# A two-layer vision transformer on one core: rounded values turned in another bank one tile later, and three queues reordered

## The chip, the cores and the metric

The kernel runs on one core of a Trainium2 chip. The metric is the device time of one execution in microseconds (us). A core has five engines with a queue each, which take their instructions in order: TensorE (PE: matrix products, and turns, that is transposes), VectorE (DVE), ScalarE (ACT), GpSimd (POOL), and SyncE (SP), which here only starts transfers. They wait for each other through semaphores. SBUF is the memory on the chip, PSUM the eight banks into which TensorE writes.

## What is computed

32 images are cut into 36 patches each and embedded; with two class tokens this makes 38 rows of 256 numbers per image. Two layers follow, each an attention and a network, with a layer norm before each:

```python
h = concat(cls_tok, cls_token, patches @ W.T + b) + pos_embedding
h = h + attn0(layernorm(h))   # a = 1 + s + s*s/2, causal, o = (a @ v) / (sum(a) + 1e-6), y = o @ Wo.T
h = h + ffn0(layernorm(h))    # x and weight rounded in blocks of 32 to a 4-bit grid, then x_q @ w_q.T + bias
h = h + attn1(layernorm(h))   # softmax attention with biases, causal, 16 heads of 16
h = h + ffn1(layernorm(h))    # gelu((x @ U1) @ V1 + b1) @ U2 @ V2 + b2
```

The rounding to the grid (per block of 32: the power of two below the largest value gives the scale, each value is rounded with the step of its own exponent) is what `scales`, `grid`, `round_to_grid` and `quantised` do for the first network, whose product is `product`.

## The kernel before

Three images make a tile of 114 rows, so there are NT = 11 tiles. Everything from the embedding on is worked tile by tile, and each engine has its own hand-written order of steps, in a function `layer0()` and a function `attention()` per engine. The loops run over tiles; at tile t an engine does steps of several stages for tiles around t. Nothing but these orders and the semaphores sets what runs when.

**First layer** (some 60 to 160 us). Per tile TensorE does `scores0(t+1)`, `values0(t)` (weights times values), `sums0(t)` (the sums of the weights, into z), `k_proj0`, `product(t-4)` of the first network, four tiles behind (LAG = 4), `v_proj0`, `q_proj0`, `out_proj0(t)` and `turn0` (the next normed tile). ScalarE does `square` (the weights), `take_z`, `add_one`, `ffn_norm(t-1)` (the norm that goes into the network), the copies `take_k0`, `take_v0`, `take_q0`, `take_hnT0` out of PSUM, and `norm0`. VectorE does `residual0(t-1)`, its half of `mask_weights(t+1)`, `divide(t)` and `ffn_residual(t-4)`; GpSimd the other half of `mask_weights` and the small steps to 1/sqrt of the variance (`rstd_0_step`, `rstd_f_step`).

The network's rounding goes by pairs of tiles p = (2p, 2p+1), six of them (NP = 6, the last has one tile). VectorE: `scales(p)` and `grid(p)`; GpSimd: `round_to_grid(p)`, two operations, and `add_ffn_bias(p)`; VectorE: `quantised(p)`, which writes the rounded values xq in bf16; TensorE: `turn_quantised(p)`; ScalarE: `take_xT(p)`, the copy from PSUM to xqT; TensorE: `product(2p)` and `product(2p+1)`; VectorE: `ffn_residual`, which adds them. In the first layer this is done for p = 0 to 3, in the second for p = 4 and 5.

The turned values of p = 0 to 3 share bank 4 with the products of `k_proj0` and `q_proj0`. So `k_proj0(t+2)` waits until they have been copied out (f_xT), and the turn stands at the end of the odd tile 2p+3:

```python
X16 = [bank[4].bitcast(bf16), bank[6].bitcast(bf16)]
pe.wait_ge(lay[0]["s_sb"], min(2 * p + 6, NT))    # in turn_quantised: q of the next tile copied out of bank 4
```

**Seam** (tiles 9 and 10 of the first layer). Instead of the next tile of the first layer, the engines do the first steps of the second: `m_proj`, `v_proj`, `s_proj` (keys, values, queries), `take_m`, `take_v`, `take_s`, `attn_norm`; GpSimd `expand(i)` (keys spread over the heads, mX) and `values_now(i)`; VectorE `keep(0)` (mask, maximum, difference) and `spread(0)`; ScalarE `weigh(0)` (the exponential). Tile i = 2 is turned into a bank that holds the values of tile 1, so that turn waits for `take_v(1)`, which waits for `values_now(0)`.

**Second layer** (some 165 to 275 us). At tile t TensorE does `scores(t+1)`, a `product`, `turn_p(t, 0..3)` (the weights, L1489), `m_proj(t+2)`, `s_proj(t+2)`, at t = 2 and 4 `turn_quantised(4)` and `(5)`, `values(t)`, `v_proj(t+2)`, `turn(t+3)`, `out_proj(t)`. VectorE does `keep(t+1)` (L1052, L1058, L1060), residuals, `spread(t+1)` (sum, reciprocal, three products L1073), `take_v(t+2)`, and the network's steps between them. `values(t)` waits for `residual(t-1)`.

## Time and profile before

| | |
|---|---|
| Time of the kernel before | 323.95 us, median of 3 runs (322.25 to 326.37) |
| The profiled execution | 326.31 us, of which the span from first to last instruction is 324.6 |
| Busy share of the span | TensorE 83%, VectorE 66%, GpSimd 53%, ScalarE 47% |
| Mean granted clock of TensorE | 0.95 of full |
| The chain that ended last | TensorE 43%, VectorE 28%, issue 9%, GpSimd 6%, ScalarE 6% |

Stages in the profiled execution: patches and embedding to 59 us, first layer to 165, second attention to 276, second network to the end. A busy share is an average over stages with different limits; which engine is waited for at the end of a stage is read from the timelines.

### The profile page before, as it was taken

Reading aid. Unit: us, or ns where it says so; the run is one execution under the profiler, and the core shown is the slowest. Engines: PE = TensorE matmul, PEld = TensorE weight load, DVE = VectorE, ACT = ScalarE, POOL = GpSimd, SP = SyncE. Lnnn points to the kernel's source line nnn. Section 1 sums busy time; section 2 is a strip of 40 time slices with the busy share of each in tenths; the row PEclk is TensorE's granted clock in tenths of the full one; section 3 lists DMA queues with packets and bytes.
Section 4 is the critical chain, followed back from the end, with each engine's and each line's share of the span. In section 5 each row is a group of like instructions: output and inputs, shape, how many; then the busy total and the mean of one; then the engine's idle time right before and its main releaser. Section 6 shows DMA issues by size and latency. Waiting matters only on the chain.

```text
span 324.6 us, 6978 instructions
## 1 busy us (share of the span) xinstructions
PE 270.3 (83%) x2720; PEld 209.0 (64%) x2720; DVE 215.1 (66%) x389; ACT 151.4 (47%) x313; POOL 171.7 (53%) x238
## 2 busy tenths in 40 slices
PE   1779899679997979798779749888999956799893
PEld 1668788558876858587668638777888844333331
DVE  0626375116698998999869998999999991422121
ACT  2312111469886858676236515543555442143541
POOL 7233335134677797979756566476776631601000
PEclk9999999799999999999979998999999995579998
DMA  6798500000000000000000000000000000001011
GB/s 178 185 267 253 128 1 3 0 0 5 2 0 2 2 2 2 1 5 0 2 0 2 2 1 3 3 0 2 0 2 2 3 0 0 3 0 31 27 60 38
DMA packets 9742, 9.87 MB, mean 30 GB/s; under 512 B 4037, under 2 KB 8878, under 8 KB 9710
## 3 DMA queue, kind: packets, MB, share of 16 engines
q1 hardware_dynamic: 9294, 9.42, 10.8%
q8 instruction: 22, 0.36, 0.5%
q14 instruction: 10, 0.08, 0.1%
q10 hardware_dynamic: 416, 0.01, 0.1%
HBM read 8.18 MB, written 1.25 MB: 29 GB/s over the span
## 4 chain that ended last, share of the span: by engine, by line
PE 43%; DVE 28%; issue 9%; POOL 6%; ACT 6%; SPq 4%; DMA 3%; ACTq 0%; POOLq 0%; DVEq 0%
PE psum L1236 8%; PE psum L1272 5%; DVE big L1073 5%; PE psum L1489 3%; PE psum L1603 3%; PE psum L1434 3%; DMA img<-in_x 3%; DVE img L988 3%; PE psum L1614 3%; SPq L323 2%; DVE st L942 2%; DVE xq L1029 2%; PE psum L1587 2%; DVE big L981 2%; PE psum L1504 2%
## 5 line engine op out<-in xcount | busy, mean ns | idle before, releaser
L1272 PE MATMUL psum<-hnT,a 128*128 128x114 f32 x352 | 50.7, 289 | 3.3 <-ACT mT L679 1.8
L1272 PEld LDWEIGHTS psum<-hnT,a 128*128 128x128 f32 x352 | 44.7, 198 | 10.1 <-ACT mT L679 4.0
L458 POOL TENSOR_SCALAR ve<-mvs 114x1 f32<-114x1 f32 x44 | 19.9, 452 | 44.4 <-DVE mvs L944 43.3
L798 ACT ACTIVATE big<-psum 114x456 f32<-114x456 f32 x44 | 22.0, 551 | 37.2 <-PE psum L1489 37.1
L1073 DVE SCALAR_TENSOR_TENSOR big<-ex,imgmask,z 114x608 f32<-114x608 f32 x33 | 34.5, 1098 | 0.4
L451 POOL TENSOR_TENSOR big<-mT,headmask 128x456 f32<-128x456 f32 x22 | 21.4, 991 | 23.9 <-ACT mT L649 23.9
L1236 PE MATMUL psum<-wT,patchT 128*114 128x256 f32 x132 | 31.8, 394 | 1.6 <-DVE patchT L898 0.8
L459 POOL TENSOR_TENSOR rstd<-ve,nhalf 114x1 f32<-114x1 f32 x44 | 30.6, 696 | 3.7
L479 POOL TENSOR_TENSOR big<-big,img 114x912 f32<-114x912 f32 x11 | 22.4, 2038 | 15.4 <-ACT big L713 15.4
L1489 PE MATMUL psum<-ident,big 114*114 114x114 f32 x176 | 22.8, 276 | 8.0 <-DVE big L1073 7.3
L1236 PEld LDWEIGHTS psum<-wT,patchT 128*114 128x114 f32 x132 | 23.8, 186 | 6.8 <-DVE patchT L898 2.1
L981 DVE SCALAR_TENSOR_TENSOR big<-big,img 114x912 f32<-114x912 f32 x11 | 16.0, 1458 | 16.4 <-ACT big L703 16.4
L1489 PEld LDWEIGHTS psum<-ident,big 114*114 114x114 f32 x176 | 19.0, 142 | 10.2 <-DVE big L1073 8.9
L703 ACT ACTIVATE big<-psum 114x912 f32<-114x912 f32 x22 | 19.3, 930 | 5.6 <-PE psum L1319 5.4
L1434 PE MATMUL psum<-big,qI 64*114 64x152 f32 x264 | 21.1, 306 | 0.6 <-POOL big L451 0.4
L1434 PEld LDWEIGHTS psum<-big,qI 64*114 64x114 f32 x264 | 18.3, 181 | 4.0 <-issue 3.4
L942 DVE BATCH_NORM_STATS2 st<-h_all 114x6 f32<-114x256 f32 x44 | 18.8, 428 | 1.5
L852 ACT ACTIVATE qc<-psum,b 128x456 f32<-128x456 f32 (+1 forms) x24 | 13.1, 606 | 13.3 <-PE psum L1603 13.3
L988 DVE RECIPROCAL img<-img 128x228 f32<-128x228 f32 x11 | 17.3, 1576 | 2.2 <-ACT img L719 1.9
L1160 DVE TENSOR_TENSOR h_all<-h_all,psum 114x256 f32<-114x256 f32 x11 | 4.5, 421 | 20.7 <-PE psum L1635 20.7
L1504 PE MATMUL psum<-big,vX 114*32 114x114 f32 x352 | 11.7, 276 | 4.5 <-DVE h_all L1083 3.8
L429 POOL TENSOR_TENSOR vX<-v_next,v_bias 114x256 f32<-114x256 f32 x11 | 8.8, 798 | 11.9 <-PE psum L1504 11.9
(158 smaller groups left out, 575.9 us busy)
## 6 DMA issues: line engine op xcount, KB each, us to landing
img<-in_x SPq DMA_DIRECT2D x6, 576.0 KB, 10.5
out<-h_all SPq DMA_DIRECT2D x10, 114.0 KB
w_raw<-in_L_tok_W SPq DMA_DIRECT2D x1, 768.0 KB, 5.9
a_raw<-in_L_attn_Wq SPq DMA_DIRECT2D x1, 256.0 KB, 8.9
a_raw<-in_L_attn_Wk SPq DMA_DIRECT2D x1, 256.0 KB, 9.0
a_raw<-in_L_attn_Wv SPq DMA_DIRECT2D x1, 256.0 KB, 9.2
a_raw<-in_L_attn_Wo SPq DMA_DIRECT2D x1, 256.0 KB, 12.7
qw<-in_L_ffn_weight SPq DMA_DIRECT2D x1, 256.0 KB, 12.8
```

Source lines behind the costliest of these rows:

```text
L451: nc.gpsimd.tensor_tensor(mX[:, c, :, :], mT[:, c:c + 1, :].to_broadcast([128, HR, T]), headmask[:, 0:HR].rearrange("p (h o) -> p h o", o= ...
L459: return nc.gpsimd.tensor_tensor(rstd[:, t:t + 1], ve[:, t:t + 1], nhalf[:, :], ALU.pow)
L479: nc.gpsimd.tensor_tensor(e, e, maskT[:, :].rearrange("p (o t) -> p o t", o=1).to_broadcast([T, H // 2, T]), ALU.mult).then_inc(e_pool, 1)
L798: nc.scalar.activation(pT[:, 4 * g:4 * g + 4, :], PTB[g % 2][0:T, 0:4 * T], ACT.Copy).then_inc(L["p"], 1)
L942: nc.vector.bn_stats(st6[:, 0, :], h_all[:, t, :]).then_inc(sums_step, 1)
L981: nc.vector.scalar_tensor_tensor(out=e, in0=e, scalar=1.0, in1=maskT[:, :].rearrange("p (o t) -> p o t", o=1).to_broadcast([T, H // 2, T]) ...
L988: step(nc.vector.reciprocal(zT[:, :, :], zT[:, :, :]))
L1073: last = nc.vector.scalar_tensor_tensor(out=pX[:, :, i, :], in0=ex[:, :, :], scalar=imgmask[:, i:i + 1], in1=z[:, :].rearrange("p (h o) -> ...
L1236: last = nc.tensor.matmul(EB[t % 2][0:T, 0:D], patchT[:, c, FIRST[t]:FIRST[t] + TI, :].rearrange("p b s -> p (b s)"), wT[:, c, :], start=( ...
L1272: return nc.tensor.matmul(bk[:, m * T:(m + 1) * T], w[:, c, m * 128:(m + 1) * 128], hnT[:, c, :], start=(c == 0), stop=(c == DC - 1))
L1434: last = nc.tensor.matmul(SB[r][0:T, c * HR * S:(c + 1) * HR * S], qI[64 * r:64 * r + 64, c, i * T:(i + 1) * T], mX[64 * r:64 * r + 64, c, ...
L1489: last = nc.tensor.transpose(PTB[g % 2][0:T, j * T:(j + 1) * T], pX[:, 4 * g + j, :, :].rearrange("p i k -> p (i k)"), ident[0:T, 0:T])
```

## The change

It does four things. (1) The turned values of p = 0 to 3 go into the upper half of bank 7, whose lower half has the products of `out_proj0` and `product`; `turn_quantised(p)` and `take_xT(p)` move from the end of tile 2p+3 into tile 2p+4, behind `sums0` and `take_z`. `k_proj0` and `m_proj` no longer wait for the copy; the turn now waits until VectorE has read the lower half. (2) VectorE in the first layer masks before it does `quantised`. (3) ScalarE does `take_k0` before `ffn_norm`; at the seam `ffn_norm(8)` and `ffn_norm(9)` go back, the latter to the end of tile 10, and `attn_norm(2)` goes ahead of `take_v(1)`. (4) In the second layer VectorE does residuals before the network's steps, `grid(4)` and `scales(5)` after `spread(2)` in tile 1, `grid(5)` in tile 2 and `quantised(5)` in tile 3; GpSimd rounds pair 5 in tile 2, not 3.

```diff
-        X16 = [bank[4].bitcast(bf16), bank[6].bitcast(bf16)]
+        X16 = [bank[7][:, D:2 * D].bitcast(bf16), bank[6].bitcast(bf16)]
...
 (GpSimd, attention)
+                    if t == 2:
+                        round_to_grid(NP - 1)
+                        add_ffn_bias(NP - 1)
                     if t == 3:
                         rstd_f_step(NT - 3)
-                        round_to_grid(NP - 1)
-                        add_ffn_bias(NP - 1)
...
 (ScalarE, layer0)
                     take_z(t)
+                    if t >= 4 and t % 2 == 0:
+                        take_xT((t - 4) // 2)
                     if t + 1 < NT:
                         add_one(t + 1)
-                    if t > 0:
-                        ffn_norm(t - 1)
                     i = t + 2 - NT
                     if i < 0:
                         take_k0(t + 2)
+                        if t > 0:
+                            ffn_norm(t - 1)
                         take_v0(t + 2)
                     else:
...
                         take_m(lay[1], i)
+                        if i == 0:
+                            ffn_norm(t - 1)
                         if i == 1:
                             weigh(lay[1], 0)
+                            attn_norm(i + 1)
                         take_v(i)
                     if i < -1:
                         norm0(t + 3)
-                    else:
+                    elif i < 1:
                         attn_norm(i + 1)
...
+                    if t == NT - 1:
+                        ffn_norm(t - 1)
                     if t < 2:
                         weight_part(t + 1)
-                    if t >= 3 and t % 2 == 1:
-                        take_xT((t - 3) // 2)
...
 (VectorE, layer0)
                     if t >= 3 and t % 2 == 1:
+                        mask_weights(t + 1)
                         quantised((t - 3) // 2)
-                        if t + 1 < NT:
-                            mask_weights(t + 1)
...
 (VectorE, attention, after keep(t + 1))
                     if t == 0:
+                        residual0(NT - 1)
                         ffn_residual(NT - 4)
-                        residual0(NT - 1)
+                    else:
+                        residual(t - 1)
                     if t == 2:
                         quantised(NP - 2)
-                    if t == 3:
-                        ffn_residual(NT - 3)
-                    if t == 4:
-                        ffn_residual(NT - 2)
-                        quantised(NP - 1)
-                    if t == 5:
-                        ffn_residual(NT - 1)
-                    if t > 0:
-                        residual(t - 1)
-                    if t == 1:
-                        grid(NP - 2)
-                    if t == 3:
-                        grid(NP - 1)
+                    if 3 <= t <= 5:
+                        ffn_residual(NT - 6 + t)
                     if t + 1 < NT:
                         spread(t + 1)
                     if t + 2 < NT:
                         take_v(t + 2)
                     if t == 0:
                         scales(NP - 2)
+                    if t == 1:
+                        grid(NP - 2)
+                        scales(NP - 1)
                     if t == 2:
-                        scales(NP - 1)
+                        grid(NP - 1)
+                    if t == 3:
+                        quantised(NP - 1)
...
 (TensorE, turn_quantised)
                 if p < NP - 2:
-                    pe.wait_ge(lay[0]["s_sb"], min(2 * p + 6, NT))
-                    ge(pe, lay[1]["s_sb"], 2 * p + 6 - NT)
+                    pe.wait_ge(lay[0]["h"], 2 * p + 4)
+                    ge(pe, f_h, 2 * p)
...
 (TensorE, layer0; k_proj0 and m_proj also lose their wait for f_xT)
                     sums0(t)
+                    if t >= 4 and t % 2 == 0:
+                        turn_quantised((t - 4) // 2)
                     if i < 0:
-                        k_proj0(t + 2, max(0, (t - 2) // 2))
+                        k_proj0(t + 2)
...
-                    if t >= 3 and t % 2 == 1:
-                        turn_quantised((t - 3) // 2)
```

What stands in a row on TensorE, from the end of tile 3 of the first layer to the product of tile 4. L1281 turns a normed tile, L1372 is `turn_quantised(0)`, L1319 scores, L1334 values, L1343 sums, L1272 (L1273 in the change) `k_proj0`, L1389 the product; of each group only its first row stands here. Before:

```order
L1281 MATMUL psum<-ident,hn 128x114 [waits L0_v_sb,L0_hnT,L0_hn]
L1372 MATMUL psum<-ident,xq 128x114 [waits L0_s_sb,f_x]
L1319 MATMUL psum<-img,mT 114x228 [waits L0_ex,L0_s_sb,L0_m_sb]
L1334 MATMUL psum<-big,vX 32x114 [waits L0_v_sb,L0_oT,e_pool,e_dve]
L1343 MATMUL psum<-big,img 32x114 x16
L1272 MATMUL psum<-hnT,a 128x114 [waits f_xT,L0_s_sb,L0_hnT]
L1389 MATMUL psum<-wq,xqT 114x256 [waits L0_h,f_xT,wq_part]
```

In the change:

```order
L1282 MATMUL psum<-ident,hn 128x114 [waits L0_v_sb,L0_hnT,L0_hn]
L1319 MATMUL psum<-img,mT 114x228 [waits L0_ex,L0_s_sb,L0_m_sb]
L1334 MATMUL psum<-big,vX 32x114 [waits L0_v_sb,L0_oT,e_pool,e_dve]
L1343 MATMUL psum<-big,img 32x114 x16
L1372 MATMUL psum<-ident,xq 128x114 [waits L0_h,f_x]
L1273 MATMUL psum<-hnT,a 128x114 [waits L0_s_sb,L0_hnT]
L1389 MATMUL psum<-wq,xqT 114x256 [waits L0_h,f_xT,wq_part]
```

The turn has moved behind scores, values and sums, and waits for a residual (L0_h) in place of the copied query.

VectorE, tile 1 of the second layer, from the difference of `keep(2)` (L1060, in the change L1066) on. Before, `residual(0)`, `grid(4)`, `spread(2)`, `take_v(3)`, then `keep(3)`:

```order
L1060 TENSOR_TENSOR sd<-sm,mx 114x608
L1083 TENSOR_TENSOR h_all<-h_all,psum 114x256
L942 BN_STATS st<-h_all 114x6
L944 BN_AGGR mvs<-st 114x2
L1020 TENSOR_TENSOR qa<-hn,rs 114x512
L869 TENSOR_SCALAR qa<-qa 114x512
L870 TENSOR_SCALAR qc<-qa 114x512
L871 TENSOR_SCALAR qc<-qc 114x512
L1068 TENSOR_REDUCE z<-ex 114x16
L1069 RECIPROCAL z<-z 114x16
L1073 SCALAR_TENSOR_TENSOR big<-ex,imgmask,z 114x16x38 x3
L1045 COPY v_next<-psum 114x256
```

In the change, from `spread(2)` (L1079) on:

```order
L1079 SCALAR_TENSOR_TENSOR big<-ex,imgmask,z 114x16x38 x3
L1051 COPY v_next<-psum 114x256
L1026 TENSOR_TENSOR qa<-hn,rs 114x512
L875 TENSOR_SCALAR qa<-qa 114x512
L876 TENSOR_SCALAR qc<-qa 114x512
L877 TENSOR_SCALAR qc<-qc 114x512
L1013 TENSOR_REDUCE am<-hn 114x8
L1014 TENSOR_SCALAR am<-am 114x8
L1015 TENSOR_SCALAR pw<-am 114x8
L1017 TENSOR_SCALAR rs<-pw,fact 114x8
L1018 RECIPROCAL rs<-rs 114x8
L1058 COPY_PREDICATED sm<-keep,psum 114x304 x2
```

`grid(4)` has moved behind `spread(2)` and `take_v(3)`, and `scales(5)`, the five small rows, now stands between it and `keep(3)`.

## Rows read from the trace of the kernel before

**Rows 1.** Windows: busy time per engine (x instructions), granted clock (PEclk), DMA.

```profile
105.00:122.00 17.00, 14.72 (x226) 12.45 (x226) 16.30 (x28) 11.78 (x23) 14.21 (x16) 1.00 0.01 2
...
166.00:168.00 2.00, 2.00 (x18) 1.87 (x16) 0.00 (x0) 0.09 (x1) 1.34 (x2) 0.50 0.00 0
```

**Rows 2.** Timeline, TensorE, first layer: start, us, operation, [idle before <-releaser].

```profile
82.91 1.15 PE L1272 MATMUL psum<-hnT,a 128*128 128x114 f32 x8 [0.22 <-ACT mT L679]
...
117.88 0.37 PE L1372 MATMUL psum<-ident,xq 114*128 114x114 bf16 x4 [1.50 <-DVE xq L1029]
...
119.97 1.00 PE L1334 MATMUL psum<-big,vX 114*32 114x114 f32 x32 [0.74 <-DVE big L981]
```

**Rows 3.** Timeline, VectorE, first layer (L1029 xq, L981 mask, L988 in divide).

```profile
98.00 2.43 DVE L1029 TENSOR_TENSOR xq<-qa,pw 114x512 bf16<-114x512 f32 x1 [0.58 <-POOL qa L489]
...
117.75 2.17 DVE L981 SCALAR_TENSOR_TENSOR big<-big,img 114x912 f32<-114x912 f32 x1
...
120.85 1.08 DVE L981 SCALAR_TENSOR_TENSOR big<-big,img 114x912 f32<-114x912 f32 x1
122.31 1.58 DVE L988 RECIPROCAL img<-img 128x228 f32<-128x228 f32 x1 [0.39 <-ACT img L719]
```

**Rows 4.** Timeline, GpSimd, first layer.

```profile
117.22 1.73 POOL L494 TENSOR_TENSOR h_all<-h_all,fbias 114x512 f32<-114x512 f32 x1
```

**Rows 5.** Timeline, ScalarE, seam (L735 ffn_norm, L639 take_v).

```profile
159.51 0.60 ACT L735 ACTIVATE hn<-h_all,shift,rstd 114x256 f32<-114x256 f32 x1 [1.94 <-POOL shift L472]
...
163.87 0.39 ACT L639 ACTIVATE v_next<-psum 114x256 f32<-114x256 f32 x1 [2.67 <-POOL vX L429]
```

**Rows 6.** Timeline, GpSimd, seam and tile 1 (L451 expand, L488 rounding, L494 bias).

```profile
160.68 1.85 POOL L451 TENSOR_TENSOR big<-mT,headmask 128x456 f32<-128x456 f32 x2 [1.20 <-ACT mT L649]
...
187.37 1.26 POOL L488 TENSOR_TENSOR qa<-qa,qc 114x512 f32<-114x512 f32 x1
...
190.36 1.80 POOL L494 TENSOR_TENSOR h_all<-h_all,fbias 114x512 f32<-114x512 f32 x1
```

**Rows 7.** Timeline, TensorE, seam to tile 3 (L1434 scores, L1489 turn_p, L1372 turn_quantised).

```profile
164.79 0.41 PE L1266 MATMUL psum<-ident,hn 114*128 114x114 f32 x2 [2.12 <-ACT hn L632]
165.33 2.94 PE L1434 MATMUL psum<-big,qI 64*114 64x152 f32 x24
...
192.87 1.56 PE L1489 MATMUL psum<-ident,big 114*114 114x114 f32 x8 [4.65 <-DVE big L1073]
...
197.91 0.37 PE L1372 MATMUL psum<-ident,xq 114*128 114x114 bf16 x4
...
201.24 1.82 PE L1434 MATMUL psum<-big,qI 64*114 64x152 f32 x24
```

**Rows 8.** Timeline, VectorE, second layer; L1052 opens keep(1) to keep(6).

```profile
168.31 0.88 DVE L1052 COPY_PREDICATED sm<-keep,psum 114x304 f32<-114x304 int32 x2 [3.12 <-PE psum L1434]
...
174.49 2.61 DVE L1073 SCALAR_TENSOR_TENSOR big<-ex,imgmask,z 114x608 f32<-114x608 f32 x3
...
178.50 0.74 DVE L1011 TENSOR_SCALAR rs<-pw,fact 114x16 f32<-114x16 f32 x1
...
179.57 0.88 DVE L1052 COPY_PREDICATED sm<-keep,psum 114x304 f32<-114x304 int32 x2
...
184.97 0.83 DVE L870 TENSOR_SCALAR qc<-qa 114x512 int32<-114x512 int32 x1
...
187.69 5.12 DVE L1073 SCALAR_TENSOR_TENSOR big<-ex,imgmask,z 114x608 f32<-114x608 f32 x3
...
193.07 0.86 DVE L1052 COPY_PREDICATED sm<-keep,psum 114x304 f32<-114x304 int32 x2
...
197.01 0.18 DVE L944 BATCH_NORM_AGGREGATE mvs<-st 114x2 f32<-114x6 f32 x1
...
204.38 0.88 DVE L1052 COPY_PREDICATED sm<-keep,psum 114x304 f32<-114x304 int32 x2
...
225.28 0.88 DVE L1052 COPY_PREDICATED sm<-keep,psum 114x304 f32<-114x304 int32 x2
```

More of the change, by code:

```diff
@@ L1283, in turn0, with k_proj0 @@
                 last.then_inc(L["hnT_ps"], 1)
-            def k_proj0(t, turned=0):
+            def k_proj0(t):
                 L = lay[0]
@@ L1288, in k_proj0 @@
                 ge(pe, L["s_sb"], t)
-                ge(pe, f_xT, turned)
                 for m in range(DC):
@@ L1391, in product, with m_proj @@
                 last.then_inc(f_y, 1)
-            def m_proj(t, turned=0):
+            def m_proj(t):
                 L = lay[1]
                 pe.wait_ge(L["hnT"], t + 1)
-                ge(pe, f_xT, turned)
                 if t == 0:
@@ L1463, in layer0 @@
                             pe.wait_ge(ld_a1, 16 * 8)
-                        m_proj(i, (t - 2) // 2)
+                        m_proj(i)
                     if t == LAG:
```

## The prediction

> **What bounds the kernel now.** The page comes first: no engine is busy for the whole span (the shares stand in the table of the profile). So the windows by stage come next. In the first layer, from 105 to 122 us, VectorE works 16.30 of 17.00 us and TensorE 14.72 [rows 1]: VectorE sets the pace. In the second layer it does so up to tile 5. From there on TensorE does: keep(6) starts at 225.28, when scores(6) end [rows 8]. The timelines then show three kinds of loss.
>
> First, TensorE waits for VectorE in every second tile of the first layer: 1.50 us for xq, then 0.74 us for the masked weights [rows 2]. VectorE itself idles only 0.39 us there, after the second mask; what it loses, it loses inside instructions. The same mask takes 2.17 us or 1.08 us [rows 3]. The long one runs while GpSimd is inside L494, which ends at 118.95; the mask ends 0.97 us later. L494 in its turn takes 1.73 us [rows 4], where L488, of the same size, takes 1.26 us [rows 6]. So an instruction that needs what the other engine holds waits for that one's end, and the two take turns. The Trainium skill ("SBUF — State Buffer", section "Who interferes with whom") states it as a rule: a VectorE instruction with two SBUF inputs, or in a 2-port mode, and a GpSimd instruction that reads SBUF exclude each other for the whole instruction. By that rule, the trace agrees.
>
> Second, the seam of the layers. ScalarE stands 1.94 us before ffn_norm(9) and 2.67 us before take_v(1) [rows 5], GpSimd 1.20 us before expand(1) [rows 6], TensorE 2.12 us before turning tile 2 [rows 7]. Then the granted clock falls to 0.50 of full, the 1.2 GHz level [rows 1], so that scores(1) take 2.94 us where scores(4) take 1.82 [rows 7]. VectorE idles 3.12 us until they are there [rows 8].
>
> Third, tile 1 of the second layer. The three spreads of tile 2 take 5.12 us; those of tile 1 took 2.61 [rows 8]. GpSimd's round_to_grid(4) and bias run beside them [rows 6]. TensorE idles 4.65 us for them, and the eight turns behind take 1.56 us [rows 7].
>
> **The change, part by part.**
>
> *First layer, take_k0 ahead of ffn_norm.* In tiles 2 and 3 TensorE waits 0.22 us each for mT [rows 2], which ScalarE copies after ffn_norm. That wait goes: **0.4 us**. ffn_norm comes later by one short copy, and VectorE reads its result in the middle of a tile.
>
> *First layer, tile 3, mask ahead of xq.* VectorE idles 0.58 us for round_to_grid(0) before the first xq [rows 3]; a mask that was ready long before now fills it. Its 0.39 us before divide(4) go as well, since the masked weights reach TensorE before xq is worked out: **1.0 us**.
>
> *First layer, tiles 5 and 7.* Both instructions stay, and so does the taking of turns: two GpSimd and two VectorE operations from 115.6 to about 120, in either order. VectorE saves the 0.39 us idle time [rows 3], less 0.1 as its last one is now the one that waited longer, in two tiles: **0.6 us**. The 2.2 us of TensorE's waits are hidden behind VectorE and bring nothing themselves. The turn in bank 7 adds a wait for residual0(t-1), which stands 0.4 us behind xq on VectorE. Queued behind a late turn are k_proj0 on TensorE, and take_xT on ScalarE with add_one(t+1) and GpSimd's mask after it. I find xq done at 120.1 and sums0 at 120.2, so the turn is some 0.3 us late, and add_one no later than now, as everything before it has moved up by 1.5 us. I take 0; the cover is thin, and a rival prices it. The three parts make **2.0 us** by the seam.
>
> *Seam.* Up to values0(10) GpSimd's queue sets the time, whatever the order of mask and xq: no change within 0.2 us. Then ffn_norm(9) leaves the front of ScalarE's queue. take_m(1) can end near 159.3, as m_proj(1) is long done, and expand(1) starts when GpSimd comes free, at 159.7, not 160.68 [rows 6]. values_now(0) then ends near 162.4 and take_s(1), behind take_v(1), near 163.3: scores(1) start at 163.4, not 165.33 [rows 7], **1.9 us** earlier. TensorE's idle stretch shrinks from 2.12 to about 1 us, so I expect the full clock, which saves scores(1) the other **1.1 us** (2.94 - 1.82). product(7) and the turns before weigh(1) ran slow too: some 0.7 us. keep(2), now at 179.57, comes **3.7 us** earlier.
>
> *Second layer, tile 1.* From keep(2) to keep(3) takes 13.50 us now [rows 8]. spread(2) moves ahead of grid(4). Its collision goes but for an ordinary 0.5: minus 2.0. The doubled tensor_scalars of grid(4) go (L870 has 0.83 us [rows 8], the others of its kind 0.43): two of them, minus 0.8. scales(5) comes in from tile 2, five small instructions, plus 1.35. It runs right behind grid(4), whose end releases GpSimd's three operations of 1.26 to 1.80 us [rows 6]. And it has three small tensor_scalars, of the kind of L1011, which took 0.74 us in one collision [rows 8]. The price of that meeting is between 0, if they slip through, and 3.3, if each waits for one GpSimd operation. I take 3.3: the two queues are released at the same moment. Sum: 13.5 - 2.0 - 0.8 + 1.35 + 3.3 = 15.4.
>
> *Tile 2.* keep(3), residual(1) and xq filled 193.07 to 197.19 [rows 8], so xq is ready 15.4 + 4.1 = 19.5 us after keep(2) starts. TensorE has its spread after about 8.5 (13.24 now, less 2.8 for grid(4) and 2.0 of collision) and is through its turns and projections at 12.2. It then idles 7 us in turn_quantised(4), with values(2), v_proj(4), out_proj(2) and scores(4) queued behind. That chain is 5.2 us at full clock (197.91 to 203.06 [rows 7]). After so long an idle stretch I add 1.4 to 2.7 us for half clock, a quarter to a half of it again; scores(1) lost six tenths of their time. keep(4) starts 26.1 to 27.4 us after keep(2), against 24.81 [rows 8]: a **loss of 1.9 us**. The wait has moved from turn_p to turn_quantised.
>
> *Tiles 3 to 5.* keep(4) to keep(6) takes 20.90 us [rows 8]. grid(5), four instructions like L870 and some 2.2 us, now lies before keep(4), and 0.3 of it is lost to TensorE's own pace: 19.0 us, **1.9 us** gained. From keep(6) on TensorE sets the pace and the gain goes to the end unchanged.
>
> **Sum.** 2.0 + 3.7 - 1.9 + 1.9 = 5.7 us. The profiled execution took 326.31 us (span 324.6), 2.4 us above the median of 323.95; the gain is taken off the median: **318.3 us**, 1.8% less. About 2% is what a measurement of this kernel can tell from no change.
>
> **Rivals.**
>
> *Scales escape GpSimd.* If the small tensor_scalars lose nothing, keep(3) comes 3.3 us sooner, TensorE idles under 4 us and keeps its clock: keep(4) starts at 22.2 after keep(2), 2.6 early instead of 1.9 late. 2.0 + 3.7 + 2.6 + 1.9 = 10.2, **313.8 us**. For it: L1011 met GpSimd once in a scales that has three such instructions. Against: three GpSimd operations are released just then.
>
> *The clock stays down in both places.* scores(1) still take 2.94 us, so keep(2) gains 2.1; the middle loses 2.6, the first layer gives 1.0: 1.0 + 2.1 - 2.6 + 1.9 = 2.4, **321.5 us**. For it: 7 us idle is more than what lowered it before.
>
> *VectorE's time is all that counts.* The instructions are the same and collisions settle elsewhere, so the edits only move waits: about 1 us, **323 us**. Against: the 3.12 us before keep(1) have a cause that goes.
>
> *Slower: ScalarE stands in take_xT.* In tiles 4, 6, 8 and 10 the turn waits for xq and a residual, take_xT for the turn, and add_one(t+1), GpSimd's mask and values0(t+1) are queued behind. If two more turns with GpSimd (1 us each, as the mask's 2.17 for 1.08) push xq back, 2.0 us in four tiles cost 8.0, and the first layer's 2.0 is lost: 323.95 - 3.7 + 8.0 = **328.2 us**. It decides from 0.9 us a tile upward (3.7 / 4). Against: GpSimd has only short operations left in those tiles.
>
> **How the numbers follow.** Forecast 0.45, scales escape 0.22, clock down 0.18, only moved 0.08, slower 0.07. The forecast's own terms leave it 316 to 320.5. The range, 313.5 to 322, reaches over the second and third case and leaves out the last two. Faster by over 2% (under 317.5): the second case and 0.4 of the first, 0.40. Slower by over 2% (over 330.4): 0.04. Within: 0.56.
>
> **What would show it.** In the first layer no wait of 1.5 us before xq's turn, and VectorE as busy as before. At the seam scores(1) in 1.82 us behind a short idle stretch. In the second layer turn_p(2) without its 4.65 us, and 4 to 7 us before the turn of xq at tile 2; tensor_scalars of 1 us and more in scales(5). The prediction is wrong if the clock is full after that wait, if ScalarE waits before take_xT in tiles 6 and 8, or if VectorE idles before divide.

## The result, and the profile after

| | before | after |
|---|---|---|
| Time, on the same chip | 323.1 us, median of 4 runs (322.06 to 326.37) | 311.3 us, median of 4 (311.12 to 311.89) |
| Ratio | | 0.962, 95% interval 0.955 to 0.970 |
| Profiled execution | 326.31, span 324.6 | 311.12, span 309.3 |
| Mean granted clock | 0.950 | 0.963 |

3.8% less: outside the range that was predicted, on the fast side. Six further runs of the changed kernel took 310.83 to 312.32; 62 runs of the kernel before, taken beside all experiments, 318.46 to 327.13. Here and below, medians and ranges are of all runs, while the ratios leave out runs more than 1.5% above the fastest of their kernel, which for xq_first are seven of ten.

The page, busy time per engine: the same work as before in a shorter span.

```profile
PE 261.0 (84%) x2720; PEld 203.4 (66%) x2720; DVE 212.2 (69%) x389; ACT 150.5 (49%) x313; POOL 171.4 (55%) x238
```

TensorE's timeline of the changed kernel (first layer, seam, tile 1, tile 2 and its chain), for [rows 2] and [rows 7]:

```profile
98.25 0.99 PE L1334 MATMUL psum<-big,vX 114*32 114x114 f32 x32 [1.34 <-issue]
...
114.10 1.00 PE L1334 MATMUL psum<-big,vX 114*32 114x114 f32 x32 [0.94 <-DVE big L987]
...
116.35 0.36 PE L1372 MATMUL psum<-ident,xq 114*128 114x114 bf16 x4 [0.47 <-DVE h_all L1002]
...
157.72 0.39 PE L1267 MATMUL psum<-ident,hn 114*128 114x114 f32 x2 [1.22 <-ACT v_next L640]
158.17 1.82 PE L1433 MATMUL psum<-big,qI 64*114 64x152 f32 x24
...
179.37 0.99 PE L1488 MATMUL psum<-ident,big 114*114 114x114 f32 x8
...
188.64 0.56 PE L1372 MATMUL psum<-ident,xq 114*128 114x114 bf16 x4 [5.54 <-DVE xq L1035]
...
190.81 2.05 PE L1418 MATMUL psum<-a,hnT 128*114 128x256 f32 x4
...
194.73 1.82 PE L1433 MATMUL psum<-big,qI 64*114 64x152 f32 x24
```

The turn of xq in the first layer waits 0.47 us for a residual where it waited 1.50 for xq. Scores(1) take 1.82 us for 2.94. `turn_p(2)` has lost its 4.65 us, and the turn of xq at tile 2 has 5.54 us that it did not have.

VectorE's timeline, for [rows 3] and [rows 8]: tile 5 of the first layer (mask, xq, second mask, divide), then keep(1), the spreads of tile 2, scales(5), keep(3), keep(4).

```profile
111.35 2.69 DVE L987 SCALAR_TENSOR_TENSOR big<-big,img 114x912 f32<-114x912 f32 x1
113.97 1.79 DVE L1035 TENSOR_TENSOR xq<-qa,pw 114x512 bf16<-114x512 f32 x1
...
116.69 1.07 DVE L987 SCALAR_TENSOR_TENSOR big<-big,img 114x912 f32<-114x912 f32 x1
117.68 1.57 DVE L994 RECIPROCAL img<-img 128x228 f32<-128x228 f32 x1
...
160.02 0.89 DVE L1058 COPY_PREDICATED sm<-keep,psum 114x304 f32<-114x304 int32 x2 [0.75 <-PE psum L1433]
...
176.12 3.03 DVE L1079 SCALAR_TENSOR_TENSOR big<-ex,imgmask,z 114x608 f32<-114x608 f32 x3
...
181.82 1.01 DVE L1014 TENSOR_SCALAR am<-am 114x8 f32<-114x8 f32 x1
...
183.08 1.11 DVE L1017 TENSOR_SCALAR rs<-pw,fact 114x8 f32<-114x8 f32 x1
...
184.46 0.88 DVE L1058 COPY_PREDICATED sm<-keep,psum 114x304 f32<-114x304 int32 x2
...
196.59 0.89 DVE L1058 COPY_PREDICATED sm<-keep,psum 114x304 f32<-114x304 int32 x2 [1.95 <-PE psum L1433]
```

The xq of tile 5 before, and GpSimd's L494 beside mask and xq in the change:

```profile
115.55 2.28 DVE L1029 TENSOR_TENSOR xq<-qa,pw 114x512 bf16<-114x512 f32 x1
...
113.03 2.18 POOL L494 TENSOR_TENSOR h_all<-h_all,fbias 114x512 f32<-114x512 f32 x1
```

The 0.39 us before divide are gone. Mask and xq together take 4.48 us in tile 5; xq and mask took 2.28 and 2.17 before. L494 takes 2.18 us for 1.73 [rows 4]. They take turns in either order; that agrees with the Trainium skill ("SBUF — State Buffer", section "Who interferes with whom"), which has whoever issues first keep the shared ports for the whole instruction. The spreads take 3.03 us for 5.12.

The windows of the changed kernel, for [rows 1]: the first layer, the stretch behind the 5.54 us, the last stage.

```profile
105.00:122.00 17.00, 15.42 (x240) 13.12 (x236) 16.38 (x29) 12.18 (x24) 14.65 (x17) 1.00 0.01 2
...
190.00:192.00 2.00, 2.00 (x23) 1.44 (x16) 2.00 (x3) 0.36 (x1) 0.92 (x2) 0.50 0.00 0
...
266.00:270.00 4.00, 3.32 (x4) 1.08 (x4) 2.23 (x5) 0.51 (x1) 2.80 (x2) 0.57 0.00 0
270.00:290.00 20.00, 18.15 (x82) 7.21 (x82) 4.70 (x11) 10.42 (x18) 2.48 (x2) 1.00 0.07 23
```

And the same last stage of the kernel before:

```profile
268.00:288.00 20.00, 15.33 (x68) 7.77 (x68) 5.26 (x13) 6.00 (x10) 6.20 (x5) 0.51 0.00 1
```

Here stands what the prediction never looked at: some 20 us at half clock, where the changed kernel has 3 to 4. TensorE's waits there are the same in both: 1.55 us before the turns of the last tile and 1.99 us before the first turn of the last network. That turn, before and in the change:

```profile
276.57 1.75 PE L1577 MATMUL psum<-ident,hn 114*128 114x114 f32 x8 [1.99 <-DVE hn L974]
...
264.12 1.17 PE L1576 MATMUL psum<-ident,hn 114*128 114x114 f32 x8 [1.99 <-DVE hn L980]
```

**Three stretches.** To compare executions I cut each at two events: the first layer's first scores, and keep(6), VectorE's step of that name in the second layer. divide(9) is VectorE's division in tile 9 of the first layer. The medians are of all runs; every other column is of one profiled execution. All in us, from the timelines.

| kernel | first scores at | from there to divide(9) | to keep(6) | keep(6) to the end | median time |
|---|---|---|---|---|---|
| before | 65.16 | 82.2 | 160.1 | 99.3 | 322.7 (62 runs) |
| after | 62.97 | 79.3 | 152.1 | 94.2 | 311.4 (10 runs) |
| again_before | 62.89 | 82.2 | 160.2 | 96.2 | 322.8 |
| again_after | 63.73 | 79.3 | 152.5 | 94.1 | 311.8 |
| m1_first_old | 64.65 | 82.2 | 153.3 | 94.5 | 316.0 |
| m2_seam_old | 62.61 | 79.3 | 152.5 | 97.2 | 316.3 |
| m3_second_old | 63.97 | 79.3 | 151.6 | 99.0 | 315.6 |
| xq_first | 64.75 | 84.4 | 155.9 | 97.3 | 320.0 |
| mask_only | 63.04 | 88.6 | 161.9 | 97.6 | 322.7 |
| s5_late | 66.90 | 80.1 | 150.5 | 94.4 | 312.0 |
| warm | 63.67 | 79.3 | 150.1 | 97.2 | 313.6 |
| tail_fill | 64.92 | 79.3 | 152.5 | 93.2 | 312.2 |
| before_tail | 62.88 | 82.2 | 160.3 | 93.3 | 317.9 |
| best | 63.42 | 79.3 | 149.7 | 92.7 | 309.7 |
| after_s8 | 63.23 | 79.3 | 152.0 | 98.1 | 315.0 |
| after_s16 | 62.95 | 79.3 | 152.0 | 97.6 | 315.6 |
| before_s8 | 63.31 | 82.2 | 160.1 | 97.1 | 321.6 |
| before_s16 | 63.38 | 82.2 | 160.1 | 96.0 | 322.6 |

The stretch to keep(6) repeats within 0.5 us between executions of the same code; what lies before and behind it does not. The change takes **8.0 us** off it (160.1 - 152.1). The rest of the 11.3 us between the medians lies in the last column and, between two single profiles, in the first.

### The profile page after: what moved, and what is told of

Read it like the earlier page. It is cut to its first block, busy times and chain, and to the rows that moved or that the text cites. A ratio compares the mean times of both kernels' runs of the same rounds, so it can differ in the third digit from the quotient of the medians.

```text
span 309.3 us, 6979 instructions
## 1 busy us (share of the span) xinstructions
PE 261.0 (84%) x2720; PEld 203.4 (66%) x2720; DVE 212.2 (69%) x389; ACT 150.5 (49%) x313; POOL 171.4 (55%) x238
## 4 chain that ended last, share of the span: by engine, by line
PE 45%; DVE 30%; issue 7%; POOL 7%; ACT 6%; DMA 3%; SPq 0%; ACTq 0%; DVEq 0%; POOLq 0%
PE psum L1237 10%; PE psum L1273 5%; PE psum L1433 4%; DVE img L994 4%; PE psum L1488 3%; DVE big L987 3%; DMA img<-in_x 3%; DVE big L1079 3%; DVE st L948 3%; PE psum L1613 3%; PE psum L1602 2%; PE psum L1503 2%; PE psum L1418 2%; PE psum L1512 2%; DVE xq L1035 2%
## 5 line engine op out<-in xcount | busy, mean ns | idle before, releaser
L1273 PE MATMUL psum<-hnT,a 128*128 128x114 f32 x352 | 48.3, 280 | 1.6 <-ACT mT L680 1.2
L1273 PEld LDWEIGHTS psum<-hnT,a 128*128 128x128 f32 x352 | 43.3, 191 | 6.1 <-ACT mT L680 1.8
L1237 PE MATMUL psum<-wT,patchT 128*114 128x256 f32 x132 | 32.7, 402 | 1.6 <-DVE patchT L904 0.8
L459 POOL TENSOR_TENSOR rstd<-ve,nhalf 114x1 f32<-114x1 f32 x44 | 31.3, 712 | 3.7
L1079 DVE SCALAR_TENSOR_TENSOR big<-ex,imgmask,z 114x608 f32<-114x608 f32 x33 | 32.3, 1031 | 0.4
L451 POOL TENSOR_TENSOR big<-mT,headmask 128x456 f32<-128x456 f32 x22 | 21.9, 1016 | 15.9 <-ACT mT L650 15.9
L1488 PE MATMUL psum<-ident,big 114*114 114x114 f32 x176 | 21.3, 263 | 2.2 <-DVE big L1079 1.6
L1433 PE MATMUL psum<-big,qI 64*114 64x152 f32 x264 | 20.0, 295 | 1.8 <-POOL big L451 1.7
L1433 PEld LDWEIGHTS psum<-big,qI 64*114 64x114 f32 x264 | 17.4, 173 | 5.4 <-issue 3.5
L1488 PEld LDWEIGHTS psum<-ident,big 114*114 114x114 f32 x176 | 17.8, 135 | 4.2 <-DVE big L1079 2.9
L429 POOL TENSOR_TENSOR vX<-v_next,v_bias 114x256 f32<-114x256 f32 x11 | 8.0, 727 | 12.6 <-PE psum L1503 12.6
```

Of the source, the lines that this page charges most:

```text
L451: nc.gpsimd.tensor_tensor(mX[:, c, :, :], mT[:, c:c + 1, :].to_broadcast([128, HR, T]), headmask[:, 0:HR].rearrange("p (h o) -> p h o", o= ...
L459: return nc.gpsimd.tensor_tensor(rstd[:, t:t + 1], ve[:, t:t + 1], nhalf[:, :], ALU.pow)
L1079: last = nc.vector.scalar_tensor_tensor(out=pX[:, :, i, :], in0=ex[:, :, :], scalar=imgmask[:, i:i + 1], in1=z[:, :].rearrange("p (h o) -> ...
L1237: last = nc.tensor.matmul(EB[t % 2][0:T, 0:D], patchT[:, c, FIRST[t]:FIRST[t] + TI, :].rearrange("p b s -> p (b s)"), wT[:, c, :], start=( ...
L1273: return nc.tensor.matmul(bk[:, m * T:(m + 1) * T], w[:, c, m * 128:(m + 1) * 128], hnT[:, c, :], start=(c == 0), stop=(c == DC - 1))
L1433: last = nc.tensor.matmul(SB[r][0:T, c * HR * S:(c + 1) * HR * S], qI[64 * r:64 * r + 64, c, i * T:(i + 1) * T], mX[64 * r:64 * r + 64, c, ...
```

## The experiments

**The two kernels again.**

> The kernel before, unchanged, profiled once more. The profiled execution of before had TensorE at half clock from 268 to 288 us, at the end of the second attention and in the last network, and ran 4.8 us longer there than the changed kernel did; it also had half clock from 59 to 63 us, worth 1.7 us. Theory A (these two stretches fall by chance with the execution, not by the program): this profile has other half-clock stretches, its span is 318 to 324, and from keep(6) to the end it can take as little as the changed kernel (94.2 us, not 99.3). Theory B (the change shifts the last stage so that its clock holds): again half clock in the last network and 99 us from keep(6) to the end. Time ratio 1.00 in both.

Measured: 322.83 (320.72 to 325.94). Its last stage is half clock for 10 us where the first profile has 20, and takes 96.2 us: neither theory's number, but the length is not fixed by the kernel.

> The changed kernel again, unchanged, for its spread and for the place of its half clock. Theory A (TensorE's half clock in the last stage comes and goes from one execution to the next, whatever the kernel): the stretch from keep(6) to the end, 94.21 us in the profiled execution of the changed kernel and 96.24 to 99.32 in the two of the kernel before, comes out between 94 and 99 here too, the single times spread over 3 to 5 us above 311, and the median of all of them moves up to 312 to 314. Theory B (the change itself keeps the clock up in the last stage): 94 to 95 us from keep(6) to the end and all times within 311 to 312.5. Up to keep(6) both expect 152.1 us from the first layer's first scores.

Measured: 311.76 (310.83 to 312.32). Theory B's numbers, not A's: the last stage takes 94.1 us in this profile and 94.2 in the first. The other eight executions have no profile; that their last stage was short too is inferred from times that all lie within 1.5 us.

**One part undone at a time** (each is the changed kernel with that part as before).

```diff
 m1_first_old:  bank 4, turn at the end of tile 2p+3, xq ahead of the mask, ffn_norm ahead of take_k0
 m2_seam_old:   ScalarE: ffn_norm(t-1) ahead of take_m, attn_norm(2) behind take_v(1)
 m3_second_old: VectorE's and GpSimd's order in attention()
```

> The changed kernel, but turn_quantised and take_xT as before (bank 4, end of the odd tile) and VectorE does xq ahead of the mask as before; take_k0 stays ahead of ffn_norm, seam and second layer as changed. My reading of the traces gives this part 2.2 us (1.3 at the first pair, 0.45 at each of two later ones): time about 313.5. Rival, VectorE's time is all that counts: 311.5. Rival, TensorE's waits of 2.2 us per pair counted in full: 317 or more.

Measured: 316.02, ratio to before 0.979 (0.969 to 0.990). 2.9 us lost at divide(9), 1.2 at keep(6). The edit is the one shown above: it also puts take_k0 back behind ffn_norm, which the expectation says it leaves. That accounts for 0.7 of the 2.9 us, and the 2.2 of the rest are what was expected there.

> The changed kernel with ScalarE's order at the seam (tiles 9 and 10) as before: ffn_norm ahead of take_m, take_v(1) ahead of attn_norm(2). My reading: scores(1) 1.9 to 2.1 us later, and if the clock falls to half there again, 1.1 to 1.6 more: 313.3 with full clock, 315 with half clock. Rival, VectorE's time is all that counts: under 1 us lost, since the same instructions remain.

Measured: 316.27, ratio 0.979 (0.972 to 0.986). TensorE's 2.12 us before the turn of tile 2 are back, but the clock stays full behind them:

```profile
159.53 0.41 PE L1263 MATMUL psum<-ident,hn 114*128 114x114 f32 x2 [2.12 <-ACT hn L633]
160.06 1.82 PE L1429 MATMUL psum<-big,qI 64*114 64x152 f32 x24
```

keep(1) comes 2.3 us later after the first scores, keep(6) 0.3.

> The changed kernel with VectorE's and GpSimd's order in the second layer as before (grid(4) ahead of spread(2), scales(5) in tile 2, quantised(5) in tile 4). My reading of the two traces gives the new order 1.4 us between keep(2) and keep(6): time about 312.8, with the three spreads of tile 2 back at 5 us, turn_p(2) waiting 4 to 5 us and the turn of xq at tile 2 not waiting. Rival, the new order removes VectorE's collisions: 3 us or more lost, 314.5.

Measured: 315.62, ratio 0.978 (0.971 to 0.985). By keep(6) the old order is 0.5 us better than the new; the median is 4 us worse, and in the profiled execution the last stage takes 99.0 us, at half clock again. So one part undone costs 4.2 to 4.9 us by the medians (none of these twelve runs is as fast as the slowest of the changed kernel's ten), but only 1.2, 0.3 and -0.5 by keep(6): what one part gains there another has in part already. In the profiles of m2_seam_old and m3_second_old the remainder sits in the last stage, 97.2 and 99.0 us. That of m1_first_old, its fastest run, has a short one (94.5), so where its other three runs lost 0.3 to 5.5 us more is not shown.

m2_seam_old tells one thing more. It comes to keep(6) 215.1 us after its first instruction, as the changed kernel does, and from there on the two run the same program; yet its last stage has half clock for at least 13 us:

```profile
258.50:271.50 13.00, 9.09 (x53) 5.48 (x51) 5.28 (x13) 1.46 (x3) 4.38 (x4) 0.50 0.01 2
```

**The square of the first layer: turn early or late, mask or xq first.** The order of take_k0 and ffn_norm, worth 0.7 us, goes with the turn: old in the two kernels with the early turn, new in the two with the late one.

```diff
 (xq_first: the changed kernel, but on VectorE; mask_only: m1_first_old with the reverse of this)
                     if t >= 3 and t % 2 == 1:
-                        mask_weights(t + 1)
                         quantised((t - 3) // 2)
+                        if t + 1 < NT:
+                            mask_weights(t + 1)
```

> The changed kernel, with VectorE's order in the first layer as it was (rounded values ahead of the next tile's mask), the turn left in bank 7 and one tile later. It separates the two halves of the first layer's part. Theory from the prediction's sum: the mask's order is what gives 1.0 us at tile 3 and 0.6 at tiles 5 and 7, the bank alone 0.4, so the seam comes 1.6 us later after the first scores, of which some 0.8 is left at keep(6); 312 to 313 us. Rival: with the turn one tile later nothing on TensorE waits for the rounded values, and the mask, one operation later, is still ahead of the scores that need it: the same time as the changed kernel within 0.5 us. Second rival: the bank is what counts, and the same holds.

Measured: 320.0 (314.76 to 320.76), ratio 0.990 (0.982 to 0.997). Far past all three expectations. Against the changed kernel it is 3.7 us worse at keep(6) and 3.1 in the last stage of its profile. TensorE's values wait in tiles 3, 5 and 7 for masked weights that are now last on VectorE, with no turn to fill the gap:

```profile
101.74 1.00 PE L1335 MATMUL psum<-big,vX 114*32 114x114 f32 x32 [3.06 <-DVE big L987]
...
119.10 1.00 PE L1335 MATMUL psum<-big,vX 114*32 114x114 f32 x32 [2.61 <-DVE big L987]
...
137.63 1.75 PE L1335 MATMUL psum<-big,vX 114*32 114x114 f32 x32 [2.26 <-DVE big L987]
```

Its windows: behind the waits at tiles 5 and 7 the clock falls, which it does in neither kernel there.

```profile
121.00:124.00 3.00, 3.00 (x21) 2.95 (x18) 2.02 (x3) 2.40 (x5) 2.00 (x5) 0.52 0.00 0
138.00:141.00 3.00, 3.00 (x67) 2.66 (x60) 1.54 (x3) 0.03 (x1) 2.56 (x5) 0.50 0.03 5
```

> The changed kernel with the bank, the turn and ScalarE's order of the first layer as they were (bank 4, turn one tile earlier), but VectorE still working the next tile's mask ahead of the rounded values: the fourth corner of a square. From the first scores to divide(9) the three known corners are 82.2 us (both old), 84.4 (turn later, old mask order) and 79.3 (both new). Theory A (the two depend on each other: the mask ahead of the rounded values helps only once nothing on TensorE waits for the rounded values soon): the early turn now stands behind the mask as well, 82 us or more, so that the whole kernel is no better than both old, 316 us or above. Theory B (the mask order is worth 5 us by itself): 77 to 79.5 us, 311 to 312 us. Theory C (the two add up, later turn -2.2, mask order 5.1): 77.1 us.

Measured: 322.69 (322.07 to 327.36), ratio 1.000 (0.997 to 1.004): theory A, and more. First layer, TensorE, then VectorE in tile 5:

```profile
99.22 0.37 PE L1374 MATMUL psum<-ident,xq 114*128 114x114 bf16 x4 [2.11 <-DVE xq L1035]
...
117.89 0.37 PE L1374 MATMUL psum<-ident,xq 114*128 114x114 bf16 x4 [3.59 <-DVE xq L1035]
```

```profile
120.27 1.11 DVE L987 SCALAR_TENSOR_TENSOR big<-big,img 114x912 f32<-114x912 f32 x1 [1.43 <-ACT big L704]
```

The early turn stands behind mask and xq both, scores0(t+1) stand behind the turn, ScalarE's square behind the scores, and VectorE's own second mask behind the square. But at tile 3 this costs nothing yet; the 6.4 us come in tiles 5 and 7 (2.7 and 3.7), and behind the waits of 3.59 us there the clock falls to half as well:

```profile
136.50:143.00 6.50, 5.08 (x80) 4.24 (x84) 3.41 (x5) 2.30 (x3) 3.23 (x7) 0.50 0.01 3
```

TensorE's values take 1.63 and 1.75 us there for 1.00. How much of the 6.4 us, and of the 2.2 of xq_first, is half clock and how much is waiting was not separated. To divide(9): both old 82.2, turn late alone 84.4, mask first alone 88.6, both 79.3. Each half of this part alone makes the first layer slower, by 2.2 (with take_k0's gain in it) and 6.4 us; together, with take_k0, they save 2.9.

**The new wait at tile 2.**

```diff
 (s5_late: VectorE, attention)
                     if t == 1:
                         grid(NP - 2)
-                        scales(NP - 1)
                     if t == 2:
+                        scales(NP - 1)
                         grid(NP - 1)
```

> The changed kernel with VectorE's scales(5) moved from the end of tile 1 to tile 2, just ahead of grid(5). Theory: the turn of the rounded values at tile 2 waits 5.54 us for VectorE's quantised(4), and scales(5) (1.01, 0.17 and 1.11 us) and the spreads of tile 2 are queued ahead of it; with 3.0 us less in the queue TensorE waits 2.5 us, its clock stays nearer to 1.0, and keep(4) comes 2 to 3.8 us earlier after the first scores than the 133.62 us of the changed kernel; about 308 us. Rival: VectorE has as much to do in either order, what leaves the queue at tile 1 comes back at tile 2 ahead of keep(4), and by keep(6) the stretch is 152.1 us as before: 311 us.

Measured: 311.97 (310.91 to 313.53). keep(6) 1.6 us earlier, no gain in the time that shows. In this profile half clock lay over the first scores and cost 0.8 us by divide(9), where the edit does nothing yet; from there to keep(6) the edit gives 2.4 us. The turn's wait fell to 2.12 us as expected:

```profile
191.52 0.37 PE L1372 MATMUL psum<-ident,xq 114*128 114x114 bf16 x4 [2.12 <-DVE xq L1035]
```

But half clock came behind it all the same, as a window shows:

```profile
194.00:196.00 2.00, 2.00 (x7) 1.34 (x6) 2.00 (x2) 0.95 (x2) 2.00 (x3) 0.50 0.02 4
```

And the collisions moved: the tile's L1066 takes 1.70 us where it took 0.79, the spreads 3.81 where they took 2.85. Part theory, part rival.

```diff
 (warm: TensorE, turn_quantised(4), ahead of the wait for xq)
+                        for _ in range(24):
+                            nc.tensor.transpose(bank[6][:, 0:128], ident[:, :], ident[:, :])
```

> The changed kernel with 24 extra turns of the unit matrix (128x128, into bank 6, which the turn behind them writes again) on TensorE ahead of its wait for the rounded values of tile 2, so that it works in 2 to 3 of the 5.54 us in which it stood; nothing else is computed. Theory: the half clock behind that wait (0.50 at 188 to 194 us) is a result of TensorE having stood; with the stretch filled the clock stays up, and values(2), the turn, the network's first products and scores(4) take 5.2 instead of some 7.6 us: keep(4) 1.9 to 2.4 us earlier after the first scores, of which 1 to 2 us is left at the end; 309 to 310 us. Rival: VectorE is busy until keep(4) whatever TensorE does: keep(4) at 133.6 us as before, 311 us. If the clock falls there all the same, what TensorE did in this one stretch is not what sets it.

Measured: 313.57 (312.69 to 316.4). TensorE:

```profile
185.16 2.78 PE L1372 MATMUL psum<-ident 128*128 128x128 f32 x24
189.59 0.37 PE L1377 MATMUL psum<-ident,xq 114*128 114x114 bf16 x4 [1.65 <-DVE xq L1035]
...
190.81 1.12 PE L1423 MATMUL psum<-a,hnT 128*114 128x256 f32 x4
...
192.93 1.82 PE L1438 MATMUL psum<-big,qI 64*114 64x152 f32 x24
```

Its windows, behind that wait and in the last stage:

```profile
188.00:195.00 7.00, 5.41 (x73) 4.37 (x74) 6.79 (x13) 3.02 (x7) 4.17 (x5) 1.00 0.01 4
256.00:271.00 15.00, 10.49 (x59) 5.96 (x56) 5.42 (x14) 2.48 (x6) 6.11 (x6) 0.54 0.01 2
```

Work that nobody reads keeps the clock at full: v_proj(4) takes 1.12 us for 2.05, keep(6) is 2.0 us earlier. Then the last stage, not touched, takes 97.2 us for 94.2, and the time is 2 us worse. The mechanism was right, the sum wrong. All four runs are slower than all ten of the changed kernel.

**The last stage.**

```diff
 (tail_fill, before_tail: TensorE; fill(n) makes n such turns of the unit matrix)
                     if t + 1 < NT:
                         scores(t + 1)
+                    else:
+                        fill(12)
...
+                    if t >= NT - 2:
+                        fill(5)
                     values(L, t)
+                    if t >= NT - 2:
+                        fill(3)
...
+            fill(15)
             ff_turn(0)
```

> The changed kernel with extra turns of the unit matrix (128x128, into bank 6, nobody reads them) on TensorE in the waits of the last two tiles of the second attention and ahead of the last network: 5 and 3 in each of the last two tiles, 12 ahead of the last tile's first turn, 15 ahead of the network's first turn. Nothing else is computed. Theory (the half clock in the last stage follows on those waits): it does not fall there, the stretch from keep(6) to the end takes 91.5 to 93 us for 94.1, so 309 to 310 us. Rival (the fall has another reason, or the extra work delays the turns behind it): 94 us or more, 311 to 313 us.

Measured: 312.18 (308.14 to 312.36). The last stage is 0.9 us shorter, less than expected, with no half clock left in it; the stage ahead of the first scores was 1.2 to 2 us longer in this profile. By the median there is no gain: 312.2 for 311.4.

> The kernel before with the same extra turns in its last two tiles and ahead of the last network. Theory (up to keep(6) the change gives 8.0 us, and what is left of the 10.9 us between the medians is half clock in the last stage, which the kernel before meets in most executions and the changed one hardly): from keep(6) to the end 91.5 to 93 us for 96.2 to 99.3, the times lie closer together than the 8 us of the kernel before, with a median of 317 to 319 us, so that it stands about 8 us behind the changed kernel with the same extra turns. Rival (the difference between the medians has another source): no less than 321 us.

Measured: 317.89 (316.88 to 318.51), ratio 0.984 (0.979 to 0.989). Its window, where the kernel before has half clock:

```profile
264.00:288.00 24.00, 20.04 (x136) 10.80 (x135) 9.17 (x22) 9.31 (x16) 8.46 (x8) 1.00 0.00 1
```

Extra work without use makes the kernel before 5 us faster; its four runs lie within 1.6 us, the 62 of before within 9. The two profiled executions with fillings differ by 5.8 us in span; with the first scores 2.0 us apart that is 7.8, the 8.0 of the stretch to keep(6). The medians (317.89 and 312.18, four runs each) differ by 5.7 us only, not by the 8 that were expected, and why is not settled.

```diff
 (after_s8, after_s16, before_s8, before_s16: TensorE, attention, tile 6; 16 for 8)
+                    if t == 6:
+                        for _ in range(8):
+                            nc.tensor.transpose(bank[6][:, 0:128], ident[:, :], ident[:, :])
                     values(L, t)
```

> The changed kernel with 8 extra turns of the unit matrix (nobody reads them) on TensorE at tile 6 of the second attention, where it has no idle time: everything behind comes 0.9 us later. Theory M (it is the moment that decides how long the half clock of the last stage lasts): the last stage, with the extra 0.9 us taken off, lasts 96 us or more instead of 94.1 in this run or in the one with 16, and the median there is 315 to 316 us. Theory C (the change itself keeps the clock up): 94.1 us with the 0.9 taken off, 312.4 us.

> The changed kernel with 16 extra turns at the same place, 1.9 us. Theory M: here or in the run with 8 the last stage is 96 us or more, less the 1.9, and the median 316 to 317 us. Theory C: 94.1 us without the 1.9, and 313.4 us.

> The kernel before with 8 extra turns at the same place. Theory M: the stretch from keep(6) to the end, 96.2 to 99.3 us and with them 0.9 more, may come out as short as 94 to 95 (without the 0.9) in this run or in the one with 16, which then is no slower than the kernel before, or faster: 320 to 322.5 us. Theory C: 96 to 99 us and 0.9 more, 323.4 us.

> The kernel before with 16 extra turns at the same place. Theory M: as for the run with 8, in one of the two 320 to 322.5 us. Theory C: 324.4 us.

Measured: 315.0, 315.59, 321.63 and 322.64 us. Less the filling, the last stage of the changed kernel lasts 97.2 and 95.7 us for 94.2, and that of the kernel before 96.1 and 94.1 for 96.2 to 99.3. A window of after_s8:

```profile
260.00:272.00 12.00, 8.10 (x49) 5.03 (x48) 5.26 (x13) 1.02 (x3) 3.95 (x4) 0.50 0.01 2
```

and one of before_s16, whose half clock ends soon:

```profile
276.00:279.00 3.00, 2.84 (x4) 1.17 (x4) 2.31 (x5) 0.00 (x0) 1.80 (x2) 0.50 0.00 0
```

Theory M holds against C: 0.9 us of extra work costs the changed kernel 3.6 us, 1.9 us cost the kernel before nothing. The short last stage goes with the moment, not with what the change does there. A rival, that the extra work by itself brings the clock down, would fit after_s8 but not before_s16: that has twice the work, and some 3 us of half clock in its last stage where before and again_before have 20 and 10. M's own number for after_s16, 316 to 317 us, was missed by 0.4 us. What the moment is counted from stays open: it is not the first instruction, as m2_seam_old shows.

**All together.** s5_late, tail_fill, and 12 turns each ahead of values(1) and of the turn at tile 2.

> The changed kernel with VectorE's scales(5) in tile 2, with extra turns ahead of TensorE's waits in values(1) (12) and at the turn of the rounded values at tile 2 (12), and with those of the last stage. Theory, added up: keep(6) at 149 to 150 us after the first scores for 152.1 (scales(5) later gave 1.6 and 24 extra turns 2.0 us by themselves, which share the same chain), 91.5 to 93 us from there to the end for 94.1: 306 to 308 us. Rival: VectorE is busy from keep(1) to keep(6) but for some 2 us, and the clock in the last stage falls again: 309 to 311 us.

Measured: 309.73 us (307.55 to 311.45), ratio to before 0.959 (0.953 to 0.964), 1.7 us under the changed kernel. The median is in the rival's range; the profiled execution (307.55), the fastest of five, is as the sum had it, 149.7 and 92.7 us, with little half clock left. From divide(9) to keep(6) it takes 70.4 us, as s5_late does, so in these two profiles the 24 turns at tiles 1 and 2 add nothing there to the late scales(5):

```profile
188.00:192.00 4.00, 4.00 (x26) 2.72 (x14) 4.00 (x4) 1.31 (x3) 3.92 (x5) 0.57 0.03 6
...
250.00:275.00 25.00, 21.04 (x176) 12.62 (x174) 12.85 (x29) 9.64 (x18) 10.67 (x10) 1.00 0.00 1
```

By its median it is the fastest that was run, though its interval overlaps that of the changed kernel.

## Why the prediction was wrong

It gave 318.3 us; ten runs have a median of 311.4. Of the 6.9 us between them 1.3 are the value it started from (323.95, a median of three, where 62 runs give 322.7), 2.3 are terms up to keep(6) that were too small, and 3.3 lie outside that stretch. Without the last the time would have been 314.7, inside the range. Gains up to keep(6), counted from the first scores:

| term | predicted | measured |
|---|---|---|
| take_k0 ahead of ffn_norm | 0.4 | 0.7 |
| tile 3 | 1.0 | 1.3 |
| tiles 5 and 7 | 0.6 | 0.9 |
| seam, to keep(2) | 3.7 | 3.7 |
| tiles 1 and 2, to keep(4) | -1.9 | -1.0 |
| tiles 3 to 5, to keep(6) | 1.9 | 2.4 |
| sum | 5.7 | 8.0 |

**The steps that held.** Where each wait would go was right: the seam to the tenth (of which 1.1 us by luck or for a reason not known, see below), scores(1) at full clock, the 4.65 us of turn_p moved to the turn of xq at tile 2 with half clock behind it, the second layer's part next to nothing in sum (0.0 predicted, 1.4 by this table, -0.5 when undone alone).

**Mis-sized: the price of scales(5).** "I take 3.3: the two queues are released at the same moment." It cost 1.7: of the three small tensor_scalars two met GpSimd, 1.01 and 1.11 us for 0.17 and 0.23, and the middle one slipped through. With that TensorE stood 5.54 us and not 7, and the loss to keep(4) was 1.0. The two ends were in the text, 0 and 3.3; the middle would have been right. The term for half clock behind the wait came out the other way: from the turn of xq to keep(4) the chain took 7.95 us for 5.15 before, 2.8 us more, just above the 1.4 to 2.7 that the prediction allowed.

**Mis-sized: the first layer**, by 0.9 in three terms, 0.3 each; why each was larger was not taken apart. "The 2.2 us of TensorE's waits are hidden behind VectorE and bring nothing themselves" fails as a statement on the parts: of the four corners of the square, only the one with both edits is fast, and the other two have TensorE's waits of 2.3 to 3.6 us in tiles 5 and 7 with half clock behind them. The slow side's rival looked at take_xT. ScalarE did wait for it, which the prediction gave as a sign of being wrong, but 0.34 us in tiles 6 and 8, and VectorE has no idle time before divide:

```profile
116.75 0.55 ACT L729 ACTIVATE xqT<-psum 128x456 bf16<-128x456 bf16 x1 [0.34 <-PE psum L1372]
```

**The step that failed: "From keep(6) on TensorE sets the pace and the gain goes to the end unchanged."** Some 20 us at half clock stood in the trace of before, from 268 to 288, and the prediction passed over them. That stretch is not a fixed cost. In the changed kernel it was 3 to 4 us: 5.1 us between the two profiles, 2.0 against again_before. before_tail shows that it is the clock (93.3 us once TensorE has no long waits there), and the kernels shifted by 0.9 and 1.9 us that the same program meets a longer or a shorter stretch of it. The 3.3 us between the medians beyond the 8.0 are of this size. That they are all of this kind is an inference, and the 5.7 us between the medians of the two kernels with fillings speak against counting on the full 8.0.

**Shown and not:** shown are the four corners of the square as measured, that TensorE's waits are needed for half clock in the last stage (filling them took it away in three kernels) and at tile 2 (24 turns took it away, 12 there and 12 at tile 1 left some 3 us), and its dependence on a shift. That a wait suffices is not so: at the seam the same 2.12 us were followed by half clock in all five profiles of the kernel before, with fillings or without, and by full clock in m2_seam_old. So the prediction's reason for the 1.1 us, a shorter idle stretch, is not shown either. Not settled: why ten times of the changed kernel lie within 1.5 us, when those of before are spread over 9, and what else than the wait decides.

## What to carry to other kernels

Two reorders that look like separate small gains can be one: here the turn gained by moving behind the values only when the mask that they wait for moved ahead, so try the corners and not only each part undone. Look at the granted clock all the way to the end, also in stages that the change doesn't touch; stretches at half clock behind TensorE's waits are part of the sum with both ends, and a difference of 1% between two orders may be no more than where such a stretch fell. Cut executions at fixed events and compare the stretch where the change works: it repeated within 0.5 us where the whole time of the kernel before was spread over 9. Start a forecast from more than three runs when the spread is of the size of the gain.

## What the runs showed of the hardware

TensorE work that nobody reads, placed in its waits, made the kernel before faster by 1.6% (317.9 for 322.7 to 323.7 us). 0.9 us of it where TensorE had no wait made the changed kernel 3.6 us slower, with longer half clock 30 us further on (after_s8). The same wait of 2.12 us was followed by half clock in five executions (before, again_before, before_s8, before_s16, before_tail) and by full clock in a sixth (m2_seam_old).
